# Linear attention with its keys first, and two expert mixtures with the deviation in the logits

## The chip, the cores and the metric

The program runs on one core of one Trainium2 chip. The metric is the time of one execution on the device, in microseconds. The engines are TensorE (PE, matrix products and transposes, with its weight loads PEld), VectorE (DVE), ScalarE (ACT), GpSimd (POOL) and the DMA queue of SyncE (SP).

## What is computed

128 rows of 256 numbers, x, pass six steps, each `x = x + step(layernorm(x))`: attention over 12544 context rows, a gated delta net, a mixture of 8 experts (the best one), a second attention over the same context, a linear attention, and a mixture of 8 experts (the best two). The change touches the two mixtures and the linear attention:

```python
# linear attention, 16 heads of 16
q, k, v = split(x @ Wqkv.T); q = elu(q) + 1; k = elu(k) + 1
decay = sigmoid(decay_param)                      # one per head
kv[t] = decay*kv[t-1] + (k*v)[t]; ksum[t] = decay*ksum[t-1] + k[t]
den = clip(sum_over_head(q * ksum), 1e-6)
out = q * kv / den
g = sigmoid(out @ Wgate.T + bgate)
return (g * out + (1 - g) * v) @ Wout.T
# second mixture; the first takes the maximum of the softmax alone
gate = softmax(x @ Wg + bg); top two, divided by their sum
return sum_e gate_e * (x @ We[e].T + be[e])
```

## The kernel before

All 128 rows lie on the 128 partitions as one tile `xres`; everything is float32 here. Each engine has its own instruction list, written out by hand, and waits on named semaphores; nothing is scheduled at run time. A layernorm (`ln_dve`, `ln_pool`, `ln_pe`, `ln_act`) runs DVE statistics, then POOL (two small operations that give `rstd`), DVE (`xn`, the deviation from the mean times `rstd`), PE (two transposes), ACT (copy to `hT`). `spin(pe, bank, n)` issues n products of the identity whose result nobody reads; each call of a float32 product of 128 columns stands in the trace as two instructions, a float32 transpose as one.

The mixture (`experts`) multiplies `hT` by eight turned expert matrices, two at a time (`product`), into four PSUM banks, while DVE works out the weights `wt`; then DVE adds the eight products to `xres` one after the other (L1548), and last the bias that PE made of `wt` and the bias rows (L1491, L1552).

The linear stage keeps channels on partitions and the 128 rows along the free axis, two blocks of 128 channels for each of q, k and v. PE projects q, k, v in six blocks (L2197). DVE and ACT make elu+1 of q and k together (L2122, L2165, L2124). DVE scans k along the rows (L2129), and PE sums q * scan over each head with the block matrix `blk16`, which leaves the same denominator on all 16 channels of a head (L2205): a tile of 128 x 256, which DVE clips and inverts (L2141, L2143). The output goes through the gate product (L2213, L2174), is mixed with v (L2148 to L2153), and is projected (L2220) and added to `xres` (L2155). Between these PE turns the expert matrices of the second mixture (`expert(i)`, four transposes each, L2186), which ACT copies out (L2161), and spins.

Of the kernel before, what the change touches and what calls it, by code (L numbers as in the profile page):

```python
# [24 lines left out]
P = 128  # L25
D = 256
# [40 lines left out]
def build(nc, a, out):  # L67
# [47 lines left out]
    with ctx:  # L115
# [1297 lines left out]
        def experts(tag, router, router_rows, router_bias, expert_bias, top, last, loads=None, clears=None, turned=None):  # L1413
# [18 lines left out]
            wt = sb(mo, "wt" + tag, [P, E])  # L1432
            wtT = rw[:, 0:P]
            n = lambda name: tag + name

            def product(pe, g):

                if last:
                    pe.wait_ge(S(n("eT")), 2 * g + 2)
                b = (5, 6, 7, 0)[g]  # L1440
                for k in range(DC):
                    ins = pe.matmul(bank[b][:], hT[:, k, :], eT[:, k, 2 * g:2 * g + 2].rearrange("p e o -> p (e o)"),  # L1442
                                    start=(k == 0), stop=(k == DC - 1))
                ins.then_inc(S(n("y")), 1)
# [22 lines left out]
            def mixture_tensor(pe):  # L1467
# [35 lines left out]
            def mixture_vector(dve):  # L1503
                ln_dve(dve, n("ln"))
                dve.wait_ge(S(n("rb_in")), 16)
                dve.wait_ge(S(n("logits_psum")), 1)
                dve.tensor_tensor(lg[:], bank[2][:, 0:E], rb[:], ALU.add).then_inc(S(n("step")), 1)
# [37 lines left out]
                dve.wait_ge(S(n("wt")), nth(n("wt")))  # L1545
                for e in range(E):
                    dve.wait_ge(S(n("y")), e // 2 + 1)
                    dve.scalar_tensor_tensor(out=xres[:], in0=bank[(5, 6, 7, 0)[e // 2]][:, (e % 2) * D:(e % 2 + 1) * D],  # L1548
                                                 scalar=wt[:, e:e + 1], in1=xres[:], op0=ALU.mult, op1=ALU.add).then_inc(S(n("step")), 1)
                    dve.wait_ge(S(n("step")), nth(n("step")))  # L1550
                dve.wait_ge(S(n("bias_psum")), 1)
                dve.tensor_tensor(xres[:], xres[:], bank[2][:, 0:D], ALU.add).then_inc(S(n("x")), 1)  # L1552
                dve.wait_ge(S(n("x")), nth(n("x")))
# [537 lines left out]
        rden = sb(la, "rden", [P, DC, P])  # L2091
# [6 lines left out]
        def linear_gpsimd(pool):  # L2098
            ln_pool(pool, "ln3")

        def linear_vector(dve):
# [18 lines left out]
            q4 = qkv[:, 0:4]  # L2120
            dve.wait_ge(S("qkv_psum"), 1)
            dve.tensor_scalar(ng[:], b4(3), 0.0, None, ALU.min).then_inc(S("ng"), 1)  # L2122
            dve.wait_ge(S("eng"), 1)
            dve.scalar_tensor_tensor(out=q4, in0=b4(3), scalar=0.0, in1=ng[:], op0=ALU.max,  # L2124
                                     op1=ALU.add).then_inc(S("phi"), 1)
            dve.wait_ge(S("phi"), 1)
            for c in range(DC):
                d = dec[:, c:c + 1].to_broadcast([P, P])
                dve.tensor_tensor_scan(scan[:, 2 + c], d, qkv[:, 2 + c], 0.0, ALU.mult, ALU.add).then_inc(S("lstep"), 1)  # L2129
                dve.wait_ge(S("lstep"), nth("lstep"))  # L2130
                dve.tensor_tensor(qs[:, c], qkv[:, c], scan[:, 2 + c], ALU.mult).then_inc(S("qs"), 1)
            dve.wait_ge(S("vl"), 1)
            dve.tensor_tensor(kvp[:], qkv[:, 2:4], qkv[:, 4:6], ALU.mult).then_inc(S("lstep"), 1)
            dve.wait_ge(S("lstep"), nth("lstep"))
            for c in range(DC):
                d = dec[:, c:c + 1].to_broadcast([P, P])
                dve.tensor_tensor_scan(scan[:, c], d, kvp[:, c], 0.0, ALU.mult, ALU.add).then_inc(S("lstep"), 1)
                dve.wait_ge(S("lstep"), nth("lstep"))
            dve.tensor_tensor(ol[:], qkv[:, 0:2], scan[:, 0:2], ALU.mult).then_inc(S("lstep"), 1)
            dve.wait_ge(S("den_psum"), 1)  # L2140
            dve.tensor_scalar(rden[:], bank[5][:, 0:D].rearrange("p (c t) -> p c t", c=DC), 1e-6, None, ALU.max).then_inc(S("lstep"), 1)  # L2141
            dve.wait_ge(S("lstep"), nth("lstep") + 1)
            dve.reciprocal(rden[:], rden[:]).then_inc(S("rden"), 1)  # L2143
            dve.wait_ge(S("rden"), nth("rden"))
            dve.tensor_tensor(ol[:], ol[:], rden[:], ALU.mult).then_inc(S("ol"), 1)
            dve.wait_ge(S("ol"), nth("ol"))

            dve.tensor_tensor(kvp[:], ol[:], qkv[:, 4:6], ALU.subtract).then_inc(S("mixstep"), 1)  # L2148
            dve.wait_ge(S("mixstep"), nth("mixstep"))
            dve.wait_ge(S("gate"), DC)  # L2150
            dve.tensor_tensor(kvp[:], kvp[:], gl[:], ALU.mult).then_inc(S("mixstep"), 1)
            dve.wait_ge(S("mixstep"), nth("mixstep"))
            dve.tensor_tensor(kvp[:], kvp[:], qkv[:, 4:6], ALU.add).then_inc(S("mixed"), 1)  # L2153
            dve.wait_ge(S("x5_psum"), 1)
            dve.tensor_tensor(xres[:], xres[:], bank[5][:, 0:D], ALU.add).then_inc(S("x5"), 1)  # L2155
# [131 lines left out]
```

## Time and profile before

| | us |
|---|---|
| median of three timed runs | 937.07 |
| the three runs | 930.34, 937.07, 938.47 |
| the profiled execution, from its first to its last instruction | 931.1 |
| PE busy, DVE busy, ACT busy, POOL busy in it | 895.8, 704.0, 487.1, 300.6 |
| first mixture with its layernorm | 544.2 to 561.0 |
| layernorm of the linear stage, end of `xn` | 899.1 |
| linear stage to the sum in `xres` (L2155) | 899.2 to 916.3 |
| second mixture to the last write of `xres` | 916.3 to 928.9 |

Of the profiled execution only this span is known; it lies inside the range of the three timed runs. Times of the stages are counted from the span's start.

### The profile page before, as it was taken

What the parts mean: (1) busy time and instruction counts of PE and PEld (TensorE: products, weight loads), DVE (VectorE), ACT (ScalarE), POOL (GpSimd) and SP (SyncE); (2) the same over time, 40 slices, a digit from 0 to 9 for tenths busy, and PEclk for the clock granted to TensorE, in tenths of its full rate; (3) what the DMA queues carried; (4) which work ended last, traced back from release to release, by engine and by line L of the source; (5) the groups of instructions that cost most, each with busy time, mean ns of one, the idle gap of its engine ahead of it and who ended that gap; (6) DMA issues with size and microseconds to landing.
All of it is one profiled execution on the core that took longest, in us unless ns stands there. A gap on an engine that the chain in (4) does not pass through costs nothing. (4 is left out here: it accounts for less than half of the span.)

```text
span 931.1 us, 21555 instructions
## 1 busy us (share of the span) xinstructions
PE 895.8 (96%) x8230; PEld 578.0 (62%) x8230; DVE 704.0 (76%) x1216; ACT 487.1 (52%) x1156; POOL 300.6 (32%) x435
## 2 busy tenths in 40 slices
PE   8999999999999999999999989999999999999887
PEld 5444554555455545666778856667777677776675
DVE  3499888988898898998576626888888888887226
ACT  2543454455435544454485313466676666676642
POOL 5563356335533653456038114400110000000100
PEclk9999999999999999999999979999999999999999
DMA  9567856584557355633210049596665677675000
GB/s 163 178 182 208 267 175 171 140 209 158 120 140 207 141 135 140 164 119 119 92 45 1 2 120 238 162 293 175 167 166 166 166 187 190 183 194 163 3 3 6
DMA packets 115080, 136.35 MB, mean 146 GB/s; under 512 B 65720, under 2 KB 86992, under 8 KB 114992
## 3 DMA queue, kind: packets, MB, share of 16 engines
q1 hardware_dynamic: 111280, 134.23, 51.8%
q10 hardware_dynamic: 3712, 0.92, 0.6%
q8 instruction: 59, 0.97, 0.5%
q14 instruction: 29, 0.24, 0.1%
HBM read 81.48 MB, written 53.07 MB: 145 GB/s over the span
## 5 line engine op out<-in xcount | busy, mean ns | idle before, releaser
L1979 DVE TENSOR_REDUCE mx<-bank 128x1 f32<-128x896 f32 x224 | 233.7, 1086 | 46.4 <-PE bank L1823 43.2
L2040 ACT ACTIVATE p<-bank 128x512 f32<-128x512 f32 x392 | 202.4, 603 | 93.6 <-PE bank L1866 93.6
L704 DVE STREAM_TRANSPOSE ew<-sc 32x896 f32<-32x896 f32 x208 | 229.3, 1102 | 15.4 <-ACT sc L788 7.7
L563 PE MATMUL bank<-Wv,ctxT 128*128 128x512 f32 (+1 forms) x336 | 146.4, 575 | 0.0
L1866 PE MATMUL bank<-home,krows 99*128 99x128 bf16 x1568 | 124.3, 220 | 6.0 <-DMA home<-n3T 2.5
L1866 PEld LDWEIGHTS bank<-home,krows 99*128 99x128 bf16 x1568 | 100.2, 98 | 44.0 <-issue 7.8
L1823 PE MATMUL bank<-krows,home 96*128 96x512 bf16 x448 | 122.2, 354 | 0.7 <-ACT home L2049 0.3
L1879 PE MATMUL bank<-p,v 128*32 128x128 f32 x3136 | 107.5, 277 | 0.8 <-issue 0.8
L563 PEld LDWEIGHTS bank<-Wv,ctxT 128*128 128x128 f32 x336 | 63.6, 190 | 71.6 <-issue 64.1
L1879 PEld LDWEIGHTS bank<-p,v 128*32 128x32 f32 x3136 | 80.5, 110 | 31.4 <-ACT p L2040 28.0
L445 POOL CAST kt<-kf 128x512 bf16<-128x512 f32 (+1 forms) x56 | 31.2, 558 | 203.3 <-ACT kf L760 203.3
L1755 POOL TENSOR_SCALAR neg<-run 128x16 f32<-128x16 f32 x14 | 3.6, 256 | 249.2 <-DVE run L1994 249.1
L543 PE MATMUL bank<-ctxT,WTk 128*128 128x512 f32 (+1 forms) x192 | 82.5, 552 | 0.7 <-ACT WTq L752 0.7
L760 ACT ACTIVATE kf<-bank,b 128x512 f32<-128x512 f32 (+1 forms) x56 | 35.6, 635 | 87.5 <-PE bank L543 86.5
L527 PE MATMUL bank<-ctxT,Wk 128*128 128x448 f32 x192 | 76.9, 545 | 1.3 <-DVE ctxT L317 1.3
L788 ACT ACTIVATE sc<-sc,neg 128x448 f32<-128x448 f32 x112 | 74.5, 668 | 0.0
L651 DVE CUSTOM_DVE_ANT_0 sc<-bank,pen 128x448 f32<-128x448 f32 x112 | 63.9, 621 | 4.7 <-issue 4.5
L775 ACT COPY v<-bank 128x256 f32<-128x256 f32 x77 | 28.7, 373 | 66.8 <-PE bank L563 66.8
L748 ACT COPY kT<-bank 128x448 f32<-128x448 f32 x56 | 29.8, 533 | 61.8 <-PE bank L527 61.8
L543 PEld LDWEIGHTS bank<-ctxT,WTk 128*128 128x128 f32 x192 | 34.5, 189 | 44.4 <-issue 37.0
L451 POOL TENSOR_TENSOR kt<-kf,kt 128x512 bf16<-128x512 f32 (+1 forms) x56 | 58.1, 1038 | 4.4
L447 POOL TENSOR_TENSOR kt<-kf,kt 128x512 bf16<-128x512 f32 (+1 forms) x56 | 58.0, 1036 | 4.5
(317 smaller groups left out, 1157.9 us busy)
## 6 DMA issues: line engine op xcount, KB each, us to landing
krows<-kscr SPq DMA_DIRECT2D x56, 384.0 KB, 6.4
krows<-kscr SPq DMA_DIRECT2D x56, 288.0 KB, 9.0
vscr<-vpair SPq DMA_DIRECT2D x12, 1004.5 KB, 4.0
kscr<-kt SPq DMA_DIRECT2D x14, 768.0 KB, 3.6
kscr<-kt SPq DMA_DIRECT2D x14, 576.0 KB, 5.1
v<-vscr SPq DMA_DIRECT2D x14, 574.0 KB, 10.8
kscr<-kt SPq DMA_DIRECT2D x14, 512.0 KB, 4.5
ctxB<-ctx SPq DMA_DIRECT2D x56, 112.0 KB, 4.0
```

The costliest lines, as they stand in the source:

```text
L451: pool.tensor_tensor(kh[:, 2, b], f, kh[:, 1, b], ALU.subtract).then_inc(S("k31"), 1)
L527: ins = pe.matmul(bank[kv_bank(op, s)][:, 0:HCH], Wk0[:, i, b * P:(b + 1) * P], turned_context(c)[:, i, half * HCH:(half + 1) * HCH], star ...
L543: ins = pe.matmul(bank[kv_bank(op, s)][:, 0:HW[half]], WTk[:, i, b * P:(b + 1) * P], turned_context(c)[:, i, HO[half]:HO[half] + HW[half]] ...
L563: ins = pe.matmul(bank[kv_bank(op, s)][:, 0:w * D], turned_context(c)[:, i, k * P:(k + 1) * P], Wv01[:, i, 0:w].rearrange("p w o -> p (w o)"),
L651: dve.tensor_tensor_reduce(out=sc0[:, s, h, half * HCH:(half + 1) * HCH], in0=bank[SX[k % 4]][:, 0:HCH], in1=pen0[:, half * HCH:(half + 1) ...
L704: dve.transpose(pT0[j * SQ:(j + 1) * SQ, :, :, i * SQ:(i + 1) * SQ].rearrange("m t h q -> m h t q"), rows[:, j]).then_inc(S("turn0"), 1)
L788: act.activation(sc0[:, s, h, cols], sc0[:, s, h, cols], ACT.Exp, bias=neg0[:, h:h + 1], accum_out=den0[:, s, h, half:half + 1]).then_inc( ...
L1823: ins = pe.matmul(bank[b + half][:, 0:HW[half]], qrows[0:KROWS, 0, h, :], krows[half][0:KROWS, r, krow(h), :], start=True, stop=True)
L1866: ins = pe.matmul(bank[ST1[g % 3]][:, i * P:(i + 1) * P], krows[half][:, c % R1, krow(h), cols], qrows[:, c % 2, h, :], start=True, stop=True)
L1879: ins = pe.matmul(bank[OT1][32 * i:32 * i + 32, j * P:(j + 1) * P], v1[:, c % R1, t, h * (D1 + 1):h * (D1 + 1) + 32], p1[:, g % PR, i * P: ...
L1979: dve.tensor_reduce(mx1[:, c % 2, h:h + 1], psum[:, b:b + 2, :].rearrange("p b n -> p (b n)")[:, 0:CH], AX.X, ALU.max).then_inc(S("smread1 ...
L2040: act.activation(p1[:, g % PR, :], bank[ST1[g % 3]][:], ACT.Exp).then_inc(S("exp1"), 1)
```

## The change

In both mixtures `xn` becomes the deviation from the mean alone; `rstd` is multiplied into the logits and into a copy of the weights, `wr`, with which the products are added. The last two experts are multiplied one at a time, the transposes of the weights and the bias product stand between them, and DVE adds the bias ahead of the last expert. In the linear stage the blocks of k are projected and treated ahead of those of q; the denominators are made with rows on partitions (128 x 16), inverted there, widened by ACT and turned back by PE; the mix becomes v plus g * (out - v), of which PE sums x (by the identity), v @ Wout and the rest in one PSUM bank, from which the second mixture reads x. The spins and the places of the experts' transposes change too. In the diff, removed lines that stand in the functions above are left out where new ones take their place.

```diff
+            wr = sb(mo, "wr" + tag, [P, E])
...
+            def y_psum(e):
+                return bank[(5, 5, 6, 6, 7, 7, 0, 1)[e]][:, e % 2 * D:(e % 2 + 1) * D]
+
+            def single_product(pe, e):
+                for k in range(DC):
+                    ins = pe.matmul(y_psum(e), hT[:, k, :], eT[:, k, e, :],
                                     start=(k == 0), stop=(k == DC - 1))
                 ins.then_inc(S(n("y")), 1)
 
...
-                for g in range(E // 2):
+                for g in range(E // 2 - 1):
                     product(pe, g)
                 pe.wait_ge(S(n("wt")), 1)
                 pe.transpose(bank[1][0:E, 0:P], wt[:], ident[:]).then_inc(S(n("wtT_psum")), 1)
+                single_product(pe, E - 2)
                 pe.wait_ge(S(n("wtT")), 1)
                 pe.wait_ge(S(n("eb_in")), 16)
                 pe.matmul(bank[2][:, 0:D], wtT[:], eb[:], start=True, stop=True).then_inc(S(n("bias_psum")), 1)
+                single_product(pe, E - 1)
...
-                ln_dve(dve, n("ln"))
+                dve.bn_stats(stats[:], x[:]).then_inc(S(n("ln_stats")), 1)
+                dve.wait_ge(S(n("ln_stats")), 1)
+                dve.bn_aggr(mv[:], stats[:]).then_inc(S(n("ln_var")), 1)
+                dve.wait_ge(S(n("ln_var")), 1)
+                dve.tensor_scalar(xn[:], x[:], mv[:, 0:1], None, ALU.subtract).then_inc(S(n("ln_xn")), 1)
+                if x is not xres:
+                    dve.tensor_copy(xres[:], x[:]).then_inc(S(n("x_copy")), 1)
                 dve.wait_ge(S(n("rb_in")), 16)
+                dve.wait_ge(S(n("ln_rstd")), 2)
                 dve.wait_ge(S(n("logits_psum")), 1)
-                dve.tensor_tensor(lg[:], bank[2][:, 0:E], rb[:], ALU.add).then_inc(S(n("step")), 1)
+                dve.scalar_tensor_tensor(out=lg[:], in0=bank[2][:, 0:E], scalar=rstd[:, 0:1], in1=rb[:], op0=ALU.mult,
+                                         op1=ALU.add).then_inc(S(n("step")), 1)
...
                 dve.tensor_scalar(wt[:], wt[:], total[:, 0:1], None, ALU.mult).then_inc(S(n("wt")), 1)
-                dve.wait_ge(S(n("wt")), nth(n("wt")))
+                dve.wait_ge(S(n("wt")), 1)
+                dve.tensor_scalar(wr[:], wt[:], rstd[:, 0:1], None, ALU.mult).then_inc(S(n("wr")), 1)
+                dve.wait_ge(S(n("wr")), 1)
+                if x is not xres:
+                    dve.wait_ge(S(n("x_copy")), 1)
                 for e in range(E):
...
+                    if e == E - 1:
+                        dve.wait_ge(S(n("bias_psum")), 1)
+                        dve.tensor_tensor(xres[:], xres[:], bank[2][:, 0:D], ALU.add).then_inc(S(n("step")), 1)
+                        dve.wait_ge(S(n("step")), nth(n("step")))
+                    dve.wait_ge(S(n("y")), e // 2 + 1 + e // (E - 1))
+                    dve.scalar_tensor_tensor(out=xres[:], in0=y_psum(e),
+                                                 scalar=wr[:, e:e + 1], in1=xres[:], op0=ALU.mult, op1=ALU.add
+                                                 ).then_inc(S(n("step" if e < E - 1 else "x")), 1)
+                    if e < E - 1:
+                        dve.wait_ge(S(n("step")), nth(n("step")))
+                dve.wait_ge(S(n("x")), 1)
...
+        den = sb(la, "den", [P, HL])
...
+
+        def two_blocks(i):
+            return bank[i][:, 0:D].rearrange("p (c t) -> p c t", c=DC)
...
-            q4 = qkv[:, 0:4]
+            q, k, v = (qkv[:, DC * i:DC * i + DC] for i in range(3))
+            eq, ek = ng[:, 0:DC], ng[:, DC:2 * DC]
             dve.wait_ge(S("qkv_psum"), 1)
...
+            dve.tensor_scalar(ek, two_blocks(3), 0.0, None, ALU.min).then_inc(S("ng"), 1)
+            dve.wait_ge(S("qkv_psum"), 2)
+            dve.tensor_scalar(eq, two_blocks(4), 0.0, None, ALU.min).then_inc(S("ng"), 1)
+            dve.wait_ge(S("exps"), 1)
+            dve.scalar_tensor_tensor(out=k, in0=two_blocks(3), scalar=0.0, in1=ek, op0=ALU.max, op1=ALU.add).then_inc(S("phi"), 1)
             dve.wait_ge(S("phi"), 1)
             for c in range(DC):
                 d = dec[:, c:c + 1].to_broadcast([P, P])
...
+                dve.tensor_tensor_scan(scan[:, 2 + c], d, k[:, c], 0.0, ALU.mult, ALU.add).then_inc(S("kscan"), 1)
+            dve.wait_ge(S("exps"), 2)
+            dve.scalar_tensor_tensor(out=q, in0=two_blocks(4), scalar=0.0, in1=eq, op0=ALU.max, op1=ALU.add).then_inc(S("phi"), 1)
+            dve.wait_ge(S("phi"), 2)
+            dve.wait_ge(S("kscan"), DC)
+            dve.tensor_tensor(qs[:], q, scan[:, 2:4], ALU.mult).then_inc(S("qs"), 1)
             dve.wait_ge(S("vl"), 1)
-            dve.tensor_tensor(kvp[:], qkv[:, 2:4], qkv[:, 4:6], ALU.mult).then_inc(S("lstep"), 1)
+            dve.tensor_tensor(kvp[:], k, v, ALU.mult).then_inc(S("lstep"), 1)
             dve.wait_ge(S("lstep"), nth("lstep"))
+            dve.wait_ge(S("den_psum"), 1)
+            dve.tensor_scalar(den[:], bank[5][:, D:D + HL], 1e-6, None, ALU.max).then_inc(S("lstep"), 1)
+            dve.wait_ge(S("lstep"), nth("lstep"))
+            dve.reciprocal(den[:], den[:]).then_inc(S("rden"), 1)
             for c in range(DC):
                 d = dec[:, c:c + 1].to_broadcast([P, P])
...
+                dve.tensor_tensor_scan(scan[:, c], d, kvp[:, c], 0.0, ALU.mult, ALU.add).then_inc(S("vscan"), 1)
+            dve.wait_ge(S("vscan"), DC)
+            dve.tensor_tensor(ol[:], q, scan[:, 0:2], ALU.mult).then_inc(S("lstep"), 1)
+            dve.wait_ge(S("lstep"), nth("lstep"))
+            dve.wait_ge(S("rden_psum"), 1)
+            dve.tensor_tensor(ol[:], ol[:], two_blocks(3), ALU.mult).then_inc(S("ol"), 1)
+            dve.wait_ge(S("ol"), 1)
+            dve.tensor_tensor(kvp[:], ol[:], v, ALU.subtract).then_inc(S("mixstep"), 1)
             dve.wait_ge(S("mixstep"), nth("mixstep"))
             dve.wait_ge(S("gate"), DC)
...
+            dve.tensor_tensor(kvp[:], kvp[:], gl[:], ALU.mult).then_inc(S("mixed"), 1)
             dve.wait_ge(S("x5_psum"), 1)
...
+            act.activation(ng[:, DC:2 * DC], ng[:, DC:2 * DC], ACT.Exp).then_inc(S("exps"), 1)
+            act.wait_ge(S("ng"), 2)
+            act.activation(ng[:, 0:DC], ng[:, 0:DC], ACT.Exp).then_inc(S("exps"), 1)
+            act.wait_ge(S("qkv_psum"), 3)
+            act.copy(qkv[:, 2 * DC:3 * DC], two_blocks(5)).then_inc(S("vl"), 1)
             expert(0)
+            act.wait_ge(S("rden"), 1)
+            act.copy(rden[:].rearrange("p (h d) -> p h d", h=HL), bc(den[:], 2, [P, HL, DL])).then_inc(S("rden_wide"), 1)
             expert(1)
...
+            def wout(k):
+                return lT[:, k, 6:8, :].rearrange("p c o -> p (c o)")
...
-            spin(pe, 6, 9)
+            spin(pe, 6, 17)
             ln_pe(pe, "ln3", 0)
             spin(pe, 6, 2)
             pe.wait_ge(S("ln3_hT"), 1)
-            for b in range(6):
...
+            for i, part in ((3, 1), (4, 0), (5, 2)):
+                for c in range(DC):
+                    for k in range(DC):
+                        ins = pe.matmul(bank[i][:, c * P:(c + 1) * P], lT[:, k, DC * part + c, :], hT[:, k, :],
+                                        start=(k == 0), stop=(k == DC - 1))
+                ins.then_inc(S("qkv_psum"), 1)
             pe.wait_ge(S("moe1ew_in"), 16)
             expert(0)
             expert(1)
-            spin(pe, 6, 7)
...
+            spin(pe, 6, 5)
+            pe.wait_ge(S("vl"), 1)
+            pe.wait_ge(S("qs"), 1)
+            for c in range(DC):
+                ins = pe.matmul(bank[5][:, D + c * (HL // DC):D + (c + 1) * (HL // DC)], qs[:, c, :],
+                                blk16[:].rearrange("p (h d) -> p h d", d=DL)[:, :, 0], start=True, stop=True)
+            ins.then_inc(S("den_psum"), 1)
+            pe.matmul(bank[4][:, 0:D], ident[:], xres[:], start=True, stop=False)
+            for k in range(DC):
+                pe.matmul(bank[4][:, 0:D], qkv[:, 2 * DC + k, :], wout(k), start=False, stop=False)
+            pe.wait_ge(S("rden_wide"), 1)
+            for c in range(DC):
+                ins = pe.transpose(bank[3][:, c * P:(c + 1) * P], rden[:, c * P:(c + 1) * P], ident[:])
+            ins.then_inc(S("rden_psum"), 1)
             expert(2)
-            expert(3)
-            spin(pe, 6, 10)
+            spin(pe, 6, 3)
             pe.wait_ge(S("ol"), 1)
             for b in range(DC):
                 for k in range(DC):
                     ins = pe.matmul(bank[6][:, b * P:(b + 1) * P], lT[:, k, 8 + b, :], ol[:, k, :],
                                     start=(k == 0), stop=(k == DC - 1))
             ins.then_inc(S("gate_psum"), 1)
+            expert(3)
             expert(4)
-            expert(5)
             pe.wait_ge(S("mixed"), 1)
             for k in range(DC):
...
+                ins = pe.matmul(bank[4][:, 0:D], kvp[:, k, :], wout(k), start=False, stop=(k == DC - 1))
             ins.then_inc(S("x5_psum"), 1)
+            expert(5)
             expert(6)
             expert(7)
-        moe1 = experts("moe1", a["L1_ffn_Wg"], False, a["L1_ffn_bg"], a["L1_ffn_be"], 2, True, turned=eT1)
```

## Rows read from the trace of the kernel before

**Rows 1.** Timeline, first mixture, 544 to 561 us (start, length, engine, line, operation, idle before).

```profile
544.25 1.62 PE L163 MATMUL bank<-ident 128*128 128x128 f32 x6 [2.38 <-PEq L83]
...
545.98 0.53 DVE L144 TENSOR_SCALAR xn<-xres,mv,rstd 128x256 f32<-128x256 f32 x1 [1.09 <-POOL rstd L151]
...
546.57 0.69 PE L157 MATMUL bank<-ident,xn 128*128 128x128 f32 x2 [0.70 <-DVE xn L144]
...
549.89 9.37 PE L1442 MATMUL bank<-home,hT 128*128 128x512 f32 x16
...
559.37 1.00 DVE L1548 SCALAR_TENSOR_TENSOR xres<-bank,wtmoe,xres 128x256 f32<-128x256 f32 x2 [0.71 <-PE bank L1442]
...
559.72 0.69 PE L1491 MATMUL bank<-ebmoe,rwmoe 8*128 8x256 f32 x2 [0.34 <-ACT rwmoe L1501]
...
560.52 0.42 DVE L1552 TENSOR_TENSOR xres<-xres,bank 128x256 f32<-128x256 f32 x1
```

**Rows 2.** TensorE by microsecond around the first mixture: busy, count, granted clock.

```profile
553.00:554.00 1.00, 1.00 (x2) 0.50 0.72 265
554.00:555.00 1.00, 1.00 (x3) 0.78 0.79 245
```

**Rows 3.** Timeline, start of the second attention, 572 to 591 us.

```profile
572.03 18.16 POOL L1791 MEMSET krows<- 3x12288 f32 x2
...
590.28 0.28 POOL L1755 TENSOR_SCALAR neg<-run 128x16 f32<-128x16 f32 x1
```

**Rows 4.** Waits by engine and releaser, 585 to 895 us (total, times, longest).

```profile
PEld bank L1866 <- DMA home<-n3T: 5.1, 12, 1.9
```

**Rows 5.** TensorE by microsecond at the start of the linear stage.

```profile
900.00:901.00 1.00, 1.00 (x7) 0.50 0.16 9
```

**Rows 6.** Timeline, linear attention, 895 to 916 us.

```profile
895.05 2.17 PE L163 MATMUL bank<-ident 128*128 128x128 f32 x18
...
899.20 0.69 PE L157 MATMUL bank<-ident,xn 128*128 128x128 f32 x2 [1.97 <-DVE xn L144]
...
903.96 0.69 DVE L2122 TENSOR_SCALAR ng<-bank 128x512 f32<-128x512 f32 x1 [4.21 <-PE bank L2197]
...
905.48 1.07 ACT L2161 COPY eT<-bank 128x512 f32<-128x512 f32 x2
906.07 0.42 DVE L2129 TENSOR_TENSOR_SCAN scan<-dec,qkv 128x128 f32<-128x128 f32 x1
...
906.57 1.28 ACT L2170 ACT_TABLE_LOAD   x1
...
909.56 1.75 DVE L2143 RECIPROCAL rden<-rden 128x256 f32<-128x256 f32 x1
...
911.83 1.16 PE L2213 MATMUL bank<-ol,home 128*128 128x128 f32 x8 [0.49 <-DVE ol L2145]
...
913.03 0.63 ACT L2174 ACTIVATE gl<-bank,bg 128x128 f32<-128x128 f32 x2 [3.73 <-PE bank L2213]
...
914.70 1.13 PE L2220 MATMUL bank<-home,kvp 128*128 128x256 f32 x4 [0.83 <-DVE kvp L2153]
...
915.66 1.04 PE L2186 MATMUL bank<-ident,ew 128*128 128x128 f32 x8
```

**Rows 7.** Timeline, second mixture, 916 to 929 us.

```profile
916.30 1.07 ACT L2161 COPY eT<-bank 128x512 f32<-128x512 f32 x2 [1.20 <-PE bank L2186]
...
916.54 1.50 PE L163 MATMUL bank<-ident 128*128 128x128 f32 x12
...
918.50 0.44 PE L157 MATMUL bank<-ident,xn 128*128 128x128 f32 x2 [0.46 <-DVE xn L144]
...
919.45 0.58 PE L1483 MATMUL bank<-rwTmoe,hT 128*128 128x8 f32 x4
...
924.09 0.23 DVE L1544 TENSOR_SCALAR wtmoe<-wtmoe,totalmoe 128x8 f32<-128x8 f32 x1
...
924.36 4.12 DVE L1548 SCALAR_TENSOR_TENSOR xres<-bank,wtmoe,xres 128x256 f32<-128x256 f32 x8
```

More of the change, by code:

```diff
@@ L1410, in build, with experts @@
         gw.close()
-        def experts(tag, router, router_rows, router_bias, expert_bias, top, last, loads=None, clears=None, turned=None):
+        def experts(tag, router, router_rows, router_bias, expert_bias, top, last, loads=None, clears=None, turned=None, x=xres):
             mo = ExitStack()
@@ L2141, in linear_vector @@
[L2141 to L2148, printed above, removed]
+                dve.tensor_tensor_scan(scan[:, c], d, kvp[:, c], 0.0, ALU.mult, ALU.add).then_inc(S("vscan"), 1)
@@ L2164, in linear_scalar @@
             act.wait_ge(S("ng"), 1)
-            act.activation(ng[:], ng[:], ACT.Exp).then_inc(S("eng"), 1)
-            act.wait_ge(S("qkv_psum"), 2)
-            act.copy(qkv[:, 4:6], bank[4][:, 0:D].rearrange("p (c t) -> p c t", c=2)).then_inc(S("vl"), 1)
+            act.activation(ng[:, DC:2 * DC], ng[:, DC:2 * DC], ACT.Exp).then_inc(S("exps"), 1)
[3 more added lines that the diff above has]
+            act.copy(qkv[:, 2 * DC:3 * DC], two_blocks(5)).then_inc(S("vl"), 1)
             expert(0)
+            act.wait_ge(S("rden"), 1)
+            act.copy(rden[:].rearrange("p (h d) -> p h d", h=HL), bc(den[:], 2, [P, HL, DL])).then_inc(S("rden_wide"), 1)
             expert(1)
@@ L2193, in linear_tensor @@
             pe.wait_ge(S("ln3_hT"), 1)
-            for b in range(6):
-                o = bank[3][:, b * P:(b + 1) * P] if b < 4 else bank[4][:, (b - 4) * P:(b - 3) * P]
-                for k in range(DC):
-                    ins = pe.matmul(o, lT[:, k, b, :], hT[:, k, :], start=(k == 0), stop=(k == DC - 1))
-                if b in (3, 5):
-                    ins.then_inc(S("qkv_psum"), 1)
+            for i, part in ((3, 1), (4, 0), (5, 2)):
+                for c in range(DC):
+                    for k in range(DC):
+                        ins = pe.matmul(bank[i][:, c * P:(c + 1) * P], lT[:, k, DC * part + c, :], hT[:, k, :],
+                                        start=(k == 0), stop=(k == DC - 1))
+                ins.then_inc(S("qkv_psum"), 1)
             pe.wait_ge(S("moe1ew_in"), 16)
@@ L2202, in linear_tensor @@
             expert(1)
-            spin(pe, 6, 7)
-            pe.wait_ge(S("qs"), DC)
-            pe.matmul(bank[5][:, 0:D], blk16[:], qs[:].rearrange("p c t -> p (c t)"), start=True,
-                      stop=True).then_inc(S("den_psum"), 1)
+            spin(pe, 6, 5)
[12 more added lines that the diff above has]
+            ins.then_inc(S("rden_psum"), 1)
             expert(2)
-            expert(3)
-            spin(pe, 6, 10)
+            spin(pe, 6, 3)
             pe.wait_ge(S("ol"), 1)
@@ L2215, in linear_tensor @@
             ins.then_inc(S("gate_psum"), 1)
+            expert(3)
             expert(4)
-            expert(5)
             pe.wait_ge(S("mixed"), 1)
             for k in range(DC):
-                ins = pe.matmul(bank[5][:, 0:D], kvp[:, k, :], lT[:, k, 6:8, :].rearrange("p c o -> p (c o)"),
-                                start=(k == 0), stop=(k == DC - 1))
+                ins = pe.matmul(bank[4][:, 0:D], kvp[:, k, :], wout(k), start=False, stop=(k == DC - 1))
             ins.then_inc(S("x5_psum"), 1)
+            expert(5)
             expert(6)
             expert(7)
-        moe1 = experts("moe1", a["L1_ffn_Wg"], False, a["L1_ffn_bg"], a["L1_ffn_be"], 2, True, turned=eT1)
+        moe1 = experts("moe1", a["L1_ffn_Wg"], False, a["L1_ffn_bg"], a["L1_ffn_be"], 2, True, turned=eT1, x=bank[4][:, 0:D])
         with nc.Block() as block:
```

26 lines of the change are left out of this document (2 added, 24 removed).

## Prediction

> **What bounds the kernel now.** I read the page first, then the waits, then the timelines of the three stretches that the diff touches, then the granted clock in them. The reader is to see four things.
>
> First, the two mixtures and the linear stage are single file: one engine works, hands over, and waits. In the first mixture TensorE begins after its spins, waits for the deviation, then needs 9.37 us for 16 instructions of the expert products, and VectorE follows with the last two additions and the bias [rows 1]. So the bound is PE's products, at half clock for their first half: the granted clock is 0.50 (1.2 GHz) up to 554 us and reaches 1.00 (2.4 GHz) in the microsecond behind it [rows 2].
>
> Second, what is gained there does reach the end: POOL fills two strips of key rows for 18.16 us as soon as the queries are picked, and the first maximum's arithmetic starts when it is through [rows 3]. That start follows from the mixture's last write by fixed work. The chunk loop behind it, 596 to 894 us, isn't touched; its only wait on a DMA of small size is that for the maxima, 5.1 us over 12 times [rows 4].
>
> Third, at the start of the linear stage PE has nothing to do for 1.97 us after its 18 spin instructions, and from the transposes on its clock is 0.50 [rows 5, 6].
>
> Fourth, the linear stage is a chain on DVE, of which the reciprocal of 128 x 256 alone is 1.75 us [rows 6]; in the second mixture it is PE's spins and then DVE (eight additions, 4.12 us) [rows 7].
>
> **First mixture.** The deviation no longer waits for rstd, a wait of 1.09 us [rows 1]. But PE's six spin instructions run from 544.25 to 545.87, and that isn't changed. So the transposes start at about 545.92 instead of 546.57: 0.65 us, and 0.4 us of the removed wait is lost behind the spins. If the clock rises at the same moment as before, products started 0.65 us earlier gain half of that, 0.33; if it rises as much earlier, 0.65. I take 0.4, near the lower end, as no row ties the rise to the start of the products. At the end: before, the last addition pair starts at 559.37, the bias product at 559.72, and the bias addition ends at 560.94, 1.57 us after the last product was let go [rows 1]. After, a transpose (0.12, as eight take 1.04) and the two instructions of the bias (0.43) stand ahead of the last product, and what follows it is one addition of 0.5. That is 1.05, a gain of 0.5. DVE is no bound: by then it has done seven additions and the bias. Sum 0.9, with ends 0.6 and 1.2.
>
> **Linear stage, clock and projections.** 34 spin instructions at 2.17/18 = 0.12 us last from 895.05 to 899.15, and xn is there at 899.14. The idle stretch is gone, so I take full clock. From transposes to the next product is then 0.95 us, as in the second mixture (918.50 to 919.45) [rows 7]: projections start at 900.15. The k blocks are eight instructions, 1.16 as for the gate [rows 6]: DVE starts at 901.35 instead of 903.96. The q blocks are there at 902.4, v at 903.3. If the clock did fall here, all of this is up to 1.3 us later.
>
> **Linear stage, DVE.** An operation on 256 columns takes 0.42 [rows 1], with the gap 0.46; so does a scan of 128 [rows 6]. Clamp k to 901.8; clamp q, which waits for PE, 902.4 to 902.85; as DVE works in order, elu of k stands behind that wait, to 903.3; two scans, 904.2; elu of q, 904.65; q * scan, 905.1. PE: projections to 903.3, eight transposes 1.04, ten spin instructions 1.2: 905.5, 0.4 us behind DVE. The denominators are four small instructions, 0.58 as for the logits [rows 7]: 906.1. Clip and invert on 128 x 16: two small operations; a small one is 0.23 [rows 7], and 1.75/16 is 0.11, so 0.4 with gaps: 906.5. Two scans, 907.4; the product with q, 907.9; times the turned reciprocal, 908.35. Beside it: ACT widens (0.4) to 906.95, PE does six instructions on 256 columns (four take 1.13 with their latency [rows 6]; six, 1.5) and two transposes (0.44), 907.7. So out is ready at 908.35, where it was 911.77.
>
> PE has four transposes and six spin instructions behind the turn: free at 908.65, 0.3 late. Gate 1.16, to 909.8; sigmoids 0.63, 910.5; one multiplication instead of two operations, 910.95. The last product starts at 911.0 instead of 914.70: **3.7 us**. ACT ahead of the sigmoids: a copy of an expert matrix 0.54 [rows 7], table load 1.28 [rows 6], another copy: free at 909.6, 0.2 ahead of the gate. That is the tightest cover here; with it gone, each 0.1 us of ACT costs 0.1.
>
> The Trainium skill (ScalarE: Activation LUTs, What ACT_TABLE_LOAD costs) says that a switch of table costs a drain of about 1.38 us beside the load of 1.28; by it the sigmoids would start 1.2 us later and this stage gain 2.5 instead of 3.7. The trace agrees on the load and shows no drain ahead of it: two copies run from 905.48 to 906.55, and the load starts at 906.57 [rows 6].
>
> **Second mixture.** Reading x in PSUM saves the addition (0.46), not waiting for rstd 1.09, as in the first. Counted from the last product's start S: statistics, aggregate and deviation are through at S + 1.15 + 0.46 + 0.2 + 0.46 = S + 2.3, where it was S + 3.75. But PE now turns three experts instead of two behind that product (0.5 more) and still spins twelve instructions (1.50): its spins began at S + 1.84, so they end at S + 2.34 + 1.5 = S + 3.84. The transposes started at S + 3.80 [rows 6, 7]. **The whole gain of the shorter layernorm is lost behind the spins**, minus 0.04. Behind that, the logits need one operation as before; `wr` is one more small operation on the path, 0.23 + 0.04 [rows 7]; the eight additions and the bias are DVE's, in any order, and PE is ahead of them: its products follow the logits (920.0) in some 7 us with the bias in between, 927.6, while the last addition starts at 924.63 + 4.12 = 928.75. The second mixture costs 0.3. The copy of x out of PSUM, 0.46 on DVE, lies beside the spins; the identity and v products for the PSUM sum lie ahead of out, as counted above. No DMA is moved: SP issues this mixture's loads after the linear stage's xn as before, and POOL's two operations for rstd (0.9) end during the spins.
>
> **Sum.** 0.9 + 3.7 - 0.3 = 4.3 us, of a span of 931.1: 926.8. The three timed runs lie 8 us apart and the profiled span lies at their lower end, so the sum goes against the median: 937.07 - 4.3 = 932.8. Less than 1% is about what a measurement of this kernel can't tell from no change, and the gain is 0.46%.
>
> **Rivals.** (a) *The shorter layernorm counts in full*: PE's spins would have to end earlier than I have them, by their being done during waits that I don't see. Then 1.5 more in the second mixture and 0.4 in the first: gain 6.2, 930.9. Against it: the spins' rows leave no room. 0.07. (b) *ACT becomes the bound of the gate*: something as long again as the table load (1.28) lies on ACT ahead of the sigmoids; with 0.2 of slack 1.1 are lost, gain 3.2, 933.9. For: the slack is small, and the widening copy holds up the copies behind it. Against: copy and load stand 0.02 us apart. 0.12. The Trainium skill's drain (the page and section above) would be such a thing. (c) *The first mixture's gain doesn't arrive*, since the second attention waits for keys, whose DMAs are issued at the same times as before: gain 3.4, 933.7. For: SP's issue doesn't depend on x. Against: POOL's fill does. 0.15. (d) *Slower*: the chunk loop starts 0.9 us earlier against gathers of keys, and the maxima's small DMAs queue behind them. Place: the wait in [rows 4], mean 0.4 us, longest 1.9. If all 12 came to the longest, 22.8 - 5.1 = 17.7 us are lost, less 4.3: 950.5. It decides the sign from a mean wait of 0.8 us. Against: the loop's issues hang on the loop's own progress and shift with it. 0.03. (e) *The same mechanism, but the median after falls in the lower group of runs* (one of three before): 930.34 - 4.3 = 926.0, faster by 1.2%. 0.14. (f) The clock falls at the linear stage's start after all (the spins end short of xn, or don't count): 1.3 lost, 934.1. 0.04.
>
> **How the numbers follow.** My forecast has 0.45, with its own range 931.6 to 933.7 from the ends 3.4 and 5.5 of the sum. With (a), (b), (c) and (f) all but 0.17 lies between 930.9 and 934.1, but three runs that lie 8 us apart don't fix a median to better than some 3 us; so 925.5 to 936.5. Faster by over 1% (under 927.7) is (e), 0.14; slower by over 1% (above 946.4) is (d), 0.03; within 1% is 0.83.
>
> **What would show each step.** PE's clock at 1.00 throughout 898 to 905; the k clamp at about 901.35 less the first mixture's 0.9; denominators as 128 x 16 and a reciprocal of about 0.2; the last product 3.7 us nearer to xn than 15.56; an idle of PE ahead of the second mixture's transposes of zero, and their distance from the last product's start still 3.8 us; in the first mixture one addition (0.5) between the last product's release and the next layernorm's statistics. The prediction fails if PE isn't found in its spins ahead of the second mixture's transposes, if the sigmoids wait for ACT, or if the loop of 596 to 894 changes its length.

## Result and the profile after

The median fell from 934.02 us (8 runs, 930.34 to 938.88) to 927.86 us (8 runs, 926.40 to 932.88): a ratio of 0.9938, 95% interval 0.9914 to 0.9962, so 3.5 to 8.0 us less. The profiled execution after has a span of 929.0 us and a time of 930.72; the one before, 931.1. Two single executions differ by 2.1 us only; the stages show why that says little:

| stage, from statistics to statistics, us | before | after |
|---|---|---|
| start of the first mixture | 544.24 | 545.99 |
| first mixture | 16.73 | 14.85 |
| second attention | 336.03 | 338.44 |
| linear stage | 19.32 | 14.41 |
| second mixture, to the last write of `xres` | 12.61 | 13.17 |

The stages that changed are 6.2 us shorter together. The stretches around them, the start and the second attention, were 4.2 us longer in this execution. Up to the start of its last product (L2220, L2269), where the prediction has its 3.7, the linear stage gained 4.46 us.

The first mixture after, in the timeline (to be held against [rows 1]):

```profile
545.99 0.91 PE L163 MATMUL bank<-ident 128*128 128x128 f32 x6 [2.38 <-PEq L83]
...
546.66 0.35 DVE L1520 TENSOR_SCALAR xn<-xres,mv 128x256 f32<-128x256 f32 x1
...
547.07 0.53 PE L157 MATMUL bank<-ident,xn 128*128 128x128 f32 x2 [0.18 <-DVE xn L1520]
...
550.24 7.31 PE L1443 MATMUL bank<-home,hT 128*128 128x512 f32 x12
...
557.39 0.27 PE L1498 MATMUL bank<-ident,wtmoe 128*8 128x128 f32 x1
...
557.50 1.03 PE L1452 MATMUL bank<-home,hT 128*128 128x256 f32 x4
...
558.46 0.69 PE L1502 MATMUL bank<-ebmoe,rwmoe 8*128 8x256 f32 x2
...
559.08 1.13 PE L1452 MATMUL bank<-home,hT 128*128 128x256 f32 x4
...
560.32 0.48 DVE L1576 SCALAR_TENSOR_TENSOR xres<-bank,wrmoe,xres 128x256 f32<-128x256 f32 x1 [0.64 <-PE bank L1452]
560.84 0.43 DVE L139 BATCH_NORM_STATS2 stats<-xres 128x6 f32<-128x256 f32 x1
...
569.79 0.38 PE L1851 MATMUL bank<-krows,home 96*128 96x512 bf16 x1 [0.77 <-DMA krows<-kscr]
```

The deviation (L1520) follows the aggregate at once, and the transposes start 1.08 us after the statistics, where it was 2.33. The spins took 0.91 us, not 1.62, since the clock fell later here: it was 0.50 from 1.3 to 8.2 us behind the statistics, and before from the statistics on for 10.2 us. One addition stands between the last product and the next statistics. The last row is new: the first scores wait for keys.

The linear stage and the second mixture (against [rows 5 to 7]):

```profile
897.33 3.96 PE L163 MATMUL bank<-ident 128*128 128x128 f32 x34
...
901.48 0.44 PE L157 MATMUL bank<-ident,xn 128*128 128x128 f32 x2 [0.19 <-DVE xn L144]
...
904.01 0.42 DVE L2155 TENSOR_SCALAR ng<-bank 128x256 f32<-128x256 f32 x1 [1.98 <-PE bank L2237]
904.46 0.42 DVE L2157 TENSOR_SCALAR ng<-bank 128x256 f32<-128x256 f32 x1
...
905.38 0.74 DVE L2163 TENSOR_TENSOR_SCAN scan<-dec,qkv 128x128 f32<-128x128 f32 x2
...
907.98 0.25 DVE L2175 RECIPROCAL den<-den 128x16 f32<-128x16 f32 x1
...
909.17 1.28 ACT L2207 ACT_TABLE_LOAD   x1
909.38 0.42 DVE L2183 TENSOR_TENSOR ol<-ol,bank 128x256 f32<-128x256 f32 x1
...
910.22 1.06 PE L2262 MATMUL bank<-ol,home 128*128 128x128 f32 x8
...
911.31 0.63 ACT L2211 ACTIVATE gl<-bank,bg 128x128 f32<-128x128 f32 x2 [0.17 <-PE bank L2262]
...
912.52 1.13 PE L2269 MATMUL bank<-home,kvp 128*128 128x256 f32 x4 [0.37 <-DVE kvp L2188]
...
913.69 0.43 DVE L1516 BATCH_NORM_STATS2 stats<-bank 128x6 f32<-128x256 f32 x1 [1.22 <-PE bank L2269]
...
914.37 0.48 DVE L1520 TENSOR_SCALAR xn<-bank,mv 128x256 f32<-128x256 f32 x1
...
914.80 1.50 PE L163 MATMUL bank<-ident 128*128 128x128 f32 x12
...
916.14 0.38 PE L157 MATMUL bank<-ident,xn 128*128 128x128 f32 x2
...
922.01 0.23 DVE L1566 TENSOR_SCALAR wrmoe<-wtmoe,rstd 128x8 f32<-128x8 f32 x1
...
922.28 3.60 DVE L1576 SCALAR_TENSOR_TENSOR xres<-bank,wrmoe,xres 128x256 f32<-128x256 f32 x7
...
926.38 0.48 DVE L1576 SCALAR_TENSOR_TENSOR xres<-bank,wrmoe,xres 128x256 f32<-128x256 f32 x1
```

The spins reach up to the transposes and the clock is 1.00 in every microsecond from 897 to 906. The reciprocal is 0.25 us instead of 1.75. From the end of `xn` to the start of the last product (L2269) it is 11.10 us, where it was 15.56. ACT's sigmoids start 0.17 us after ACT is free. In the second mixture the deviation ends at 914.85, and the transposes follow the spins without a gap, 1.3 us later.

### The profile page after: what moved, and what is told of

Read it like the earlier page. It is cut to its first block and busy times, and to the rows that moved or that the text cites. A ratio compares the mean times of both kernels' runs of the same rounds, so it can differ in the third digit from the quotient of the medians.

```text
span 929.0 us, 21593 instructions
## 1 busy us (share of the span) xinstructions
PE 895.1 (96%) x8246; PEld 579.0 (62%) x8246; DVE 703.2 (76%) x1218; ACT 487.8 (53%) x1158; POOL 300.9 (32%) x435
```

## Experiments

Each is measured against runs of the kernel before on the same chip, on three chips in all (e1 to e4; e5 and e7 to e9; e6 and e10 to e12). The changed kernel wasn't timed again beside them, so a difference between two ratios carries both intervals, and each of them overlaps with the changed kernel's. "Stage" is the length in the one profile of that kernel, as in the table above. The wait of PE for keys at the first scores, and the time from the first mixture's statistics to those scores, come from the same profile.

| kernel | ratio to before, 95% | first mixture | to first scores (wait) | linear | second mixture |
|---|---|---|---|---|---|
| before | 1 | 16.73 | 24.99 (0) | 19.32 | 12.61 |
| changed | 0.9914 to 0.9962 | 14.85 | 23.80 (0.77) | 14.41 | 13.17 |
| first mixture old | 0.9946 to 0.9997 | 16.25 | 24.50 (0) | 14.41 | 13.15 |
| first mixture alone | 0.9953 to 0.9994 | 14.86 | 23.11 (0) | 17.97 | 12.62 |
| 9 spins | 0.9933 to 0.9973 | 16.14 | 24.39 (0) | 16.04 | 13.15 |
| no spins, 2nd mixture | 0.9918 to 0.9962 | 14.58 | 23.31 (0.55) | 14.40 | 12.19 |
| wide denominators | 0.9927 to 0.9965 | 14.62 | 22.87 (0) | 15.92 | 13.17 |
| q and k together | 0.9934 to 0.9968 | 13.04 | 23.60 (2.37) | 15.72 | 13.17 |
| sums by DVE | 0.9943 to 0.9978 | 14.65 | 24.17 (1.33) | 15.21 | 12.70 |
| maxima first | 0.9942 to 0.9972 | 12.03 | 24.25 (4.03) | 14.41 | 13.17 |
| bias last | 0.9908 to 0.9957 | 14.61 | 22.92 (0) | 14.41 | 13.17 |
| wr directly | 0.9913 to 0.9960 | 14.69 | 23.47 (0.59) | 14.41 | 12.96 |
| keys early | 0.9877 to 0.9931 | 12.02 | 21.29 (1.08) | 14.40 | 13.17 |
| combined | 0.9881 to 0.9934 | 12.96 | 21.21 (0) | 14.41 | 12.01 |

**First mixture as before in the changed kernel, and alone in the kernel before (e1, e2).** The edit is `moe0 = experts(...)` with the old or the new function.

> The changed kernel with its first mixture as before (layernorm waits for rstd, products in four pairs, bias last); linear stage and second mixture changed. In the two profiles the first mixture went from 16.73 to 14.85 us (from its statistics to the next layernorm's), but the second attention behind it from 336.0 to 338.4. Theory A (gains of the first mixture reach the end, 0.9 forecast): this kernel is about 1 to 2 us slower than the changed one, 4.3 to 5 us faster than before. Theory B (the second attention starts against transfers that are no earlier, and takes the gain back): the same time as the changed kernel, about 6 us faster than before, with no wait for keys at its first scores. Linear stage 14.4 us and second mixture 13.2 in either.

> The kernel before with only the first mixture changed. Theory A: 1 to 2 us faster than before. Theory B: no difference, the first mixture shorter by 0.9 to 1.9 us in the profile and the second attention longer by as much, with a wait for keys at its first scores (0.8 us in the changed kernel) or for the maxima ahead of its second chunk (1.0 before, 2.2 changed). Linear stage 19.3 us and second mixture 12.6 as before.

Ratios 0.9972 and 0.9973. The two halves add up: 2.6 us (0.3 to 5.0) for the linear stage with the second mixture, 2.5 us (0.6 to 4.4) for the first mixture alone. So the first mixture's gain does reach the end, in good part: in the profiles with the new one (keys early and combined left out) the first scores come 22.9 to 24.4 us after the mixture's statistics, with or without a wait for keys, and 24.5 to 25.0 with the old one. Theory A holds. The 2.5 is over twice the 0.9 forecast, but the interval doesn't exclude 0.9; what the profiles say of the size is told below.

**Fewer spins ahead of the linear stage (e3).**

```diff
-            spin(pe, 6, 17)
+            spin(pe, 6, 9)
```

> The changed kernel with 9 instead of 17 spin calls ahead of the linear layernorm's transposes. If the longer spins keep the clock: PE idle for 2 us, then granted 0.50 for some 3.3 us, transposes and the k blocks late by 0.25 + 0.4 + 0.7 = 1.3 us, the q blocks then behind the k clamp; linear stage 15.7 us or more instead of 14.4. If they don't matter: 14.4 us, clock 1.00.

```profile
900.38 0.44 PE L157 MATMUL bank<-ident,xn 128*128 128x128 f32 x2 [1.97 <-DVE xn L144]
...
901.27 4.58 PE L2237 MATMUL bank<-hT,home 128*128 128x128 f32 x24
...
905.00 0.42 DVE L2157 TENSOR_SCALAR ng<-bank 128x256 f32<-128x256 f32 x1 [0.84 <-PE bank L2237]
```

The clock fell to 0.50 about 1 us after PE's idle of 1.97 had ended, all 24 projections took 4.58 us instead of 2.94, the q clamp waited for them, and the stage was 16.04: the cover is worth 1.6 us when the clock falls. It doesn't always: in the profile of the first mixture alone the old stage with 9 spins, and the same idle of 1.97, ran at 1.00 throughout and took 17.97, not 19.32. At full clock on both sides the linear stage thus gained 3.56 us of the 4.91; the other 1.35 are the fall.

**No spins ahead of the second mixture's transposes (e4).**

```diff
-                spin(pe, 3 if last else 7, 6 if last else 3)
+                if not last:
+                    spin(pe, 7, 3)
```

> The changed kernel without the twelve spin instructions ahead of the second mixture's transposes. My theory: PE's spins, not the layernorm, set their start, so they start as soon as the deviation is there or the three experts are turned, 1.1 us earlier, and the second mixture ends 1.1 us earlier (12.1 instead of 13.2 us), if ACT has copied the experts by then: its eighth copy ends at 915.68, so the copy of hT behind it would be 0.8 instead of 1.2 us earlier, and the gain 0.8. Rival: the clock falls without them, and the products lose 0.5 us or more; then no gain.

```profile
908.14 1.13 PE L2270 MATMUL bank<-home,kvp 128*128 128x256 f32 x4 [0.37 <-DVE kvp L2189]
...
910.00 0.48 DVE L1521 TENSOR_SCALAR xn<-bank,mv 128x256 f32<-128x256 f32 x1
...
910.63 0.41 PE L157 MATMUL bank<-ident,xn 128*128 128x128 f32 x2
```

The transposes start with the turned experts and the deviation, 2.49 us after the last product's start instead of 3.62, and the mixture is 0.98 us shorter: here the spins, not the layernorm, set the time. The ratio, 0.9940, can't tell it from the changed kernel.

**The denominators as before (e7)** (blk16 as weights, DVE clips and inverts 128 x 256, no widening, no turn).

```diff
-                ins = pe.matmul(bank[5][:, D + c * (HL // DC):D + (c + 1) * (HL // DC)], qs[:, c, :], ...
+            ins = pe.matmul(bank[5][:, D:2 * D], blk16[:], qs[:].rearrange("p c t -> p (c t)"), ...
```

> The changed kernel with the denominators as before: 128 x 256 from the block matrix, clipped and inverted by DVE, no widening copy and no transposes; v product and residual stay in PSUM. If the 128 x 16 denominators are what the linear stage gained most by: DVE's clip and reciprocal take 0.42 + 1.75 instead of 0.17 + 0.25, all on its chain, so out is ready 1.7 us later, less whatever the narrow form lost on the way (PE's wait for the widened copy: none seen); linear stage 16.0 instead of 14.4 us. Rival: the turn through ACT and PE costs as much as it saves, 14.4 to 14.8 us.

15.92: the narrow form is worth 1.51 us of the stage. The reciprocal was 1.75 again.

**q and k together (e8).** One clamp, one exponential and one sum on four blocks.

> The changed kernel with q and k clamped, raised and summed together on 512 columns, as before, q projected first. In the changed kernel the k clamp starts 0.45 us ahead of the q clamp, and q's sum runs behind the scans. If keys first is worth something: q * scan is ready 0.8 us later, linear stage 15.1 to 15.2 instead of 14.4 us. Rival: the two extra operations cost what the overlap gives, since DVE works in order; 14.4 to 14.6 us.

15.72: keys first is worth 1.31 us, more than the 0.8 expected. Most of it is the start: the clamp, which now waits for the blocks of k too, starts 3.52 us behind `xn` instead of 2.59. Another 0.43 is lost up to q * scan (6.41 instead of 5.05), where one pass on 512 columns leaves ACT and DVE waiting for each other.

**v and x added by DVE (e9).** `kvp + v` and `xres + bank[4]` come back, the identity and v products go.

> The changed kernel with v added by DVE, x added by DVE into SBUF, and the second mixture reading x there. The first addition lies on the path (0.46): linear stage up to the last product 0.46 longer. The second (0.46) lies ahead of the layernorm, which is hidden behind PE's spins (the deviation is ready at S + 2.3, the spins end at S + 3.6, S being the last product's start). So, if the spins hold, only 0.46 is lost in all up to the second mixture's transposes, not 0.92; and PE has six instructions of 256 columns fewer ahead of the gate, of which nothing comes back if DVE sets out's time. Rival: 0.9 lost.

Linear stage 0.80 longer, second mixture 0.47 shorter: 0.33 net, where 0.46 was expected. The addition ahead of the layernorm was hidden behind the spins, as expected.

**Maxima first (e5).**

```diff
-            for r in (1, 2):
-                sp.wait_ge(S(f"vscr_late{r}"), 16)
-                fetch_values(sp, r)
+            sp.wait_ge(S("vscr_late1"), 16)
+            fetch_values(sp, 1)
...
                     rows(c + 1)
+                if c == 0:
+                    sp.wait_ge(S("vscr_late2"), 16)
+                    fetch_values(sp, 2)
```

> The changed kernel with the load of the third chunk's values issued behind the second chunk's maxima instead of ahead of them. In the changed kernel's profile the three small transfers of the maxima took 4.1 us instead of 1.7 to land there, PE waited 2.2 us and its clock then fell to 0.50 for 3.5 us; before, PE waited 1.0 us. If they queue behind the values: the wait goes to zero or some tenths, second attention 1 to 2 us shorter than 336 us, and the spread of the runs shrinks, as no clock falls there. Rival: the queue there is that of the key gathers, and nothing changes, or the later values hold up the third chunk (a wait at about 640 us).

PE's timeline at the second chunk, the changed kernel and then this one:

```profile
618.29 0.61 PE L1894 MATMUL bank<-home,krows 99*128 99x128 bf16 x8 [2.21 <-issue]
```

```profile
616.45 0.61 PE L1896 MATMUL bank<-home,krows 99*128 99x128 bf16 x8 [0.30 <-issue]
```

The wait went from 2.21 to 0.30 and no clock fell there. It is likely but not shown that the edit did it: the profile names no releaser, and the wide-denominator kernel had 0.42 there without this edit. Its ratio, 0.9957, shows no gain. One reason stands in its profile: some 14 us later PE waited 2.29 us for keys, and no other profile has a wait of 0.9 us or more there; eight loads of keys are now issued behind two of the values (615.95 behind 614.85). The gain moved into another wait, as the rival had it. The other reason is no matter of the edit. In this execution the clock stayed at 1.00 in the first mixture, which took 12.03 us, and then PE stood waiting for keys:

```profile
567.88 0.91 PE L1853 MATMUL bank<-krows,home 96*128 96x512 bf16 x2 [4.03 <-DMA krows<-kscr]
...
632.72 0.54 PE L1853 MATMUL bank<-krows,home 96*128 96x512 bf16 x2 [2.29 <-DMA krows<-kscr]
```

The clock fell in the last microsecond of those 4.03 us, and was 0.50 up to 573.6. A faster first mixture runs into the keys' landing and pays twice.

**Keys early (e11).** The decay and gate-bias loads go behind `gather(sp, 0, 0)` and `gather(sp, 0, 1)` in `l1_loads`.

> The changed kernel with the three small loads of the linear stage (decay twice, gate bias; 1.8 us of the queue's issuing) behind the first chunk's keys instead of ahead of them. So far the first scores never start earlier than 22.9 us after the first mixture's statistics, and PE waits there for keys by 0.5 to 4.0 us wherever the mixture took under 14.9 us. If the keys' landing is the floor: no wait for keys there, or one that is 1.8 us shorter than the mixture's length would give; a gain of 0.5 to 1 us where the clock falls in the mixture, more where it doesn't. Rival: the landing is set by bandwidth, not by the issue, and the floor stays at 23 to 24 us.

The first mixture took 12.02 us again, and the scores started at 21.29, after 1.08 us of waiting, against 24.25 with 4.03. The six profiles with the old issue that wait for keys have 23.31 to 24.25, so the floor moved by 2.0 to 3.0 us with the issue: issue sets it, not bandwidth alone. Ratio 0.9904.

**Bias last in both mixtures (e10).** `product` for all four pairs, then the transpose and the bias.

> The changed kernel with the experts in four pairs and the bias added last in both mixtures; the deviation stays in the logits. First mixture: my sum gave the reordering 0.5 us of it, so 15.3 to 15.4 instead of 14.85 us (with the clock falling as in the other profiles). Second mixture: DVE's nine additions set the end in any order, 13.17 us as it is. Rival: in the second the bias is late when it comes last, and it is longer by 0.2 or more.

```profile
550.72 8.49 PE L1443 MATMUL bank<-home,hT 128*128 128x512 f32 x16
...
559.32 1.00 DVE L1570 SCALAR_TENSOR_TENSOR xres<-bank,wrmoe,xres 128x256 f32<-128x256 f32 x2 [0.71 <-PE bank L1443]
...
560.92 0.43 DVE L139 BATCH_NORM_STATS2 stats<-xres 128x6 f32<-128x256 f32 x1
```

14.61 and 13.17: the reordering is worth next to nothing in either. From the moment DVE can add the last product to the next statistics it is 1.60 us here and 0.52 in the new order (560.32 to 560.84 above), but that moment is 1.05 us later behind the transpose and the bias: the last additions are let go 9.65 us after the first product's start in the profile without spins, whose clock rose 3.1 us behind that start, and 8.60 us after it here, where it rose after 2.8. Half of that difference in the rise, 0.11 us, is clock, which leaves 0.94.

**wr made directly (e6).**

```diff
+                dve.tensor_scalar(wr[:], wt[:], total[:, 0:1], rstd[:, 0:1], ALU.mult, ALU.mult).then_inc(S(n("wr")), 1)
                 dve.tensor_scalar(wt[:], wt[:], total[:, 0:1], None, ALU.mult).then_inc(S(n("wt")), 1)
-                dve.wait_ge(S(n("wt")), 1)
-                dve.tensor_scalar(wr[:], wt[:], rstd[:, 0:1], None, ALU.mult).then_inc(S(n("wr")), 1)
```

> The changed kernel with wr made of the unscaled weights in one operation (times 1/sum, times rstd) and issued ahead of wt. The path loses one small operation: 0.27 us less in the second mixture (12.90 instead of 13.17), nothing in the first, where PE's products set the end. Rival: wt, now behind wr, holds up the transpose and the bias: no gain.

12.96 instead of 13.17: 0.21 us. Not to be told apart by time (0.9937).

**Combined (e12).**

> The changed kernel with three edits together: no spins ahead of the second mixture's transposes, wr made directly, the three small loads behind the first keys. Sum of the parts: second mixture 13.17 - 0.98 - 0.27 = 11.9 us, linear stage 14.4 us, the first scores without a wait for keys; 1.2 to 2.5 us faster than the changed kernel, ratio to before about 0.991 to 0.993. Rival: the second mixture's parts overlap (ACT's hT copy or the logits set the path) and give 1.0 together.

12.01 and 14.41, no wait for keys. Ratio 0.9907, the same as keys early alone (0.9904); 0.3% better than the changed kernel, with intervals that overlap.

## Why the prediction was right, and where it wasn't

The forecast was 4.3 us less, 0.46%, by the linear stage above all; measured were 6.2 us in the medians and 0.38% to 0.86% by the interval. The direction, a gain of under 1%, and the account of the linear stage and of the second mixture's spins were right. The time itself, 932.8, was not met: 927.86 lies inside the wide range (925.5 to 936.5) and outside my own (931.6 to 933.7). Of the 4.9 us between, 3.05 are the median before, 937.07 of three runs and 934.02 of eight, and 1.9 the gain. The ends 3.4 and 5.5 of the sum, on which my own range stood, were worked out from nothing in the prediction.

*Linear stage.* 3.7 us were forecast to the last product, 4.46 came out against the profile before, in which the clock had fallen; against that of the first mixture alone, whose old stage ran at full clock (14.21 from `xn` to the last product), it is 3.11. The order of the steps was right. My start was too early (the k clamp came 2.59 us after `xn`, not 2.21) and my run of DVE too slow: two scans without a wait between them take 0.74, not 0.9, and the q clamp came straight behind the k clamp. The narrow denominators gave 1.51, where 1.6 was expected ahead of that run. What I left out is that the kernel before doesn't always pay the fall; the half with this stage is worth 2.6 us in time.

*Second mixture.* Transposes at S + 3.84 forecast, S + 3.62 measured; `wr` 0.27, measured 0.29 between the transposes and the end (10.43 and 10.72). From S to the end the stage costs 0.11 us (14.23 and 14.34), 0.3 forecast. The claim that the shorter layernorm is lost behind the spins was shown by taking them away (0.98). So rival (a) is out as a mechanism, and that the medians lie 6.2 us apart, the very number it gave, is chance. (b) is out too: the table load stands 0.02 us behind its copy, and 0.17 us of slack was left of the 0.2 forecast. The drain that the Trainium skill (ScalarE: Activation LUTs, What ACT_TABLE_LOAD costs) puts beside the load shows in none of the profiles.

*First mixture.* The term of 0.9 was mis-sized, in both its parts. The reordering of the bias, 0.5 in my sum, is nothing in the profiles (e10), and 0.1 with the clock's part taken out: I priced transpose and bias at 0.55, and they push the last addition back by about 1. The deviation, 0.4 in my sum, is the rest, and its size hangs on where the half clock lies.

In the profile before, the clock was 0.50 for 10.2 us from the statistics on, and the mixture took 16.73. The 9-spins profile has as much half clock, from 0.2 us behind the statistics. Its products start 1.17 us earlier (4.48, not 5.65), and the mixture took 16.14: half of the earlier start comes through, as I had it for a rise at the same moment. The other old one (e1) was 0.50 for 6.8 us, from 3.0 to 9.9 us behind the statistics, and took 16.25. Seven new ones were 0.50 for the same 6.8 us, but it ended 7.2 to 8.3 us behind the statistics, and they took 14.58 to 14.86. Bias last is one of them and differs from e1 in the first mixture by the deviation alone: its products start 0.63 us earlier (4.41, not 5.04), and from their start to the last pair of additions it is 8.60, not 9.61. That 1.01 is clock: of the same 6.8 us, 4.9 lie on the products in e1 and 2.8 in bias last. I had reckoned with a rise at the same moment or as much earlier as the start; here it came 2.7 us earlier, since the fall did. Of the last four, two had 3.4 us of half clock (13.0) and two none (12.0).

The mean granted clock points the same way: 0.9919 in 80 runs of the ten kernels with the new first mixture (keys early and combined left out), 0.9895 in the 12 runs of e1, 0.9893 in 58 of the kernel before. The 0.0024 between the first two, at 9.4 us for 0.01 (below), is 2.3 us. Whether the change moves the fall, or executions differ in it by themselves, isn't shown: the old mixture has two profiles only.

*Rival (c)* is true in part. Keys are there some 23 to 24 us after the mixture's statistics, and PE waits for them by 0.5 to 4 us where the mixture is short; but 1 to 2 us arrive. From the end of the mixture to the first maximum's product (L1831, L1859) it is 30.7 to 30.8 us in the seven profiles without such a wait, and 31.44 in the changed kernel's, with its 0.77. *Rival (d)* exists in small: in twelve of the fourteen profiles PE waits 1.0 to 2.2 us for the maxima of the second chunk (1.04 in the profile before, 2.21 in the one after), with a fall of the clock behind it in seven. It is no cost of the change: the profile with the old first mixture has a wait of 1.95. The loop, whose change in length I had named as a sign of failure, is 305.3 us before and 307.0 after from that product to the linear stage's statistics; but it is 302.9 to 309.0 over all profiles, with the same instructions in all but e5, so the sign tells nothing.

*Rival (e)*, a median in the lower group, is what the time looks like (927.86), but the runs lie in no groups; see below.

## What to carry to other kernels

Ask what stands beside a step before pricing its removal: the narrow denominators were worth nearly their full price (1.51 us) on DVE's bare chain, and the shorter layernorm of the second mixture nothing while PE still had spins in front. Spins that keep the clock are part of the schedule: after a cut they must be recounted, each call is 0.23 us, or they become the bound. A stage made faster collides with the next one's loads; moving three small loads behind the keys took the wait from 4.03 us to 1.08 in two profiles with an equally short mixture, and the ratio may be better for it (0.9904 against 0.9938, intervals that overlap).

## What the runs showed of the hardware

The spread of the runs is in the main time at half clock. Over the 32 runs of the kernel before on one chip, time and mean granted clock go together with a correlation of -0.86, 9.4 us for each 0.01: 940.86 us at 0.985, 930.75 at 0.996. A loss of 0.01 of the span's 931 us is 9.3 us of it, so there nearly every one of them reaches the end. On the two other chips the 15 and 11 runs give 6.9 and 8.7 us, with correlations of -0.75 and -0.73. The places are few: 500 us, the barrier ahead of the first mixture, the keys' wait, the second chunk's maxima, the maxima at 875 us (three profiles, behind waits of 1.6 to 2.3 us), the linear stage's start. Whether the clock falls at a given gap differs from one execution to the next of the same instructions: the gap of 1.97 us ahead of the linear layernorm's transposes cost it in the profile before and with 9 spins, and not in that of the first mixture alone; after the barrier's 2.4 us it held in two profiles. The Trainium skill (TensorE: Matmul & The Clock Gate, Part 1) calls the number of slow products at the start of a kernel run-variable and the ramp's penalty under 1% of a typical span. Here the runs of one kernel lie 1.1% apart, in the main by falls of the clock in mid-kernel, which is more than this change is worth.

A transpose of the weights and the two bias instructions put between float32 products, the last pair of which was split in two, held the last addition up by 1.05 us (9.65 against 8.60), 0.94 without the clock's part, where their own lengths as I had them make 0.55. By the starts in the changed kernel's first mixture the transpose takes 0.11 (557.39 to 557.50) and the bias 0.62 (558.46 to 559.08), so 0.73. The first of the two single products takes 0.96; half a pair at full clock is 0.87 in the second mixture (three pairs from 917.47 to 922.70), so the splitting costs 0.09 for each, if the second is like the first. That makes 0.91 of the 0.94.
